# Value tiles copied out of PSUM by ScalarE, the x1 spread moved to ScalarE and its maxima to the next body

## What is computed

```python
x = x + tanh(g_xattn) * mha(layernorm(x), ctx, ctx, Wq, bq, Wk, bk, Wv, bv, Wo, bo)
x = x + tanh(g_ffn)   * ffn(layernorm(x), clip_x, clip_down, w_gate, w_up, w_down)

# mha: v = ctx @ Wv.T + bv;  o = softmax(q k / sqrt(32)) @ v;  result = o @ Wo.T + bo
# ffn: xq = fake_quant(x, clip_x)      scale = sigmoid(clip_x) * max|x| / 127 over the whole tensor
#      h  = fake_quant(silu(xq @ Wg.T) * (xq @ Wu.T), clip_down);  result = h @ Wd.T
```

## Time and profile before

| what | value |
|---|---|
| median of three runs | 1910.21 us (1909.71 to 1914.14) |
| the profiled execution | 1910.74 us, its span 1909.0 us |
| busy over the span | PE 88%, DVE 76%, ACT 45%, POOL 26% |
| granted TensorE clock, mean | 0.970 |
| chain that ended last | issue 38%, PE 31%, DVE 16%, POOL 8%, DMA 5%, ACT 2% |
| costliest lines of VectorE | L842 304.4 us (256), L834 224.6 us (128) |
| start, 14 steady bodies, body 15 and last body, weights, feed-forward | to 107; to 1211; to 1336; to 1383; to the end |

### The profile page before, as it was taken

How to read it: one execution, slowest core, us unless ns; L and a number is a source line. 1 busy time by engine, 2 the same in 40 slices (tenths; PEclk the granted TensorE clock), 3 DMA queues, 4 the chain that set the end, 5 groups by cost and what they waited for, 6 DMA issues and landing times.

```text
span 1909.0 us, 36308 instructions
## 1 busy us (share of the span) xinstructions
PE 1687.6 (88%) x12892; PEld 832.0 (44%) x12892; DVE 1441.6 (76%) x1917; ACT 866.3 (45%) x1036; POOL 497.3 (26%) x686
## 2 busy tenths in 40 slices
PE   3788999989999899998999989986599999989787
PEld 3354444544445444454444444433344444434333
DVE  6648788787786877868778687777877778878555
ACT  2243433434335343353443533414777777756242
POOL 6123323223232232322323223212000000006634
PEclk6999999999999999999999999999799999999899
DMA  5233332323323233233332332225235454115897
GB/s 187 67 109 92 88 105 73 110 87 88 109 81 101 87 86 112 84 94 105 84 100 85 91 107 61 78 56 199 94 121 210 165 203 150 45 45 213 337 419 296
DMA packets 132189, 239.73 MB, mean 126 GB/s; under 512 B 17456, under 2 KB 66608, under 8 KB 129584
## 3 DMA queue, kind: packets, MB, share of 16 engines
q1 hardware_dynamic: 132144, 239.14, 38.1%
HBM read 126.10 MB, written 62.39 MB: 99 GB/s over the span
## 4 chain that ended last, share of the span: by engine, by line
issue 38%; PE 31%; DVE 16%; POOL 8%; DMA 5%; ACT 2%; POOLq 0%; DVEq 0%; SPq 0%; ACTq 0%
PE bank L1244 11%; PE bank L1149 5%; PE bank L1151 5%; PE bank L1150 5%; PE spair L1226 4%; DMA x<-out_dram 4%; DVE mx L842 3%; POOL xl L485 3%; DVE rs L834 3%; POOL yh L559 3%; DVE xbuf L806 2%; DVE v L826 1%; ACT xh L580 1%; DVE ndev L866 1%; DVE parts L821 1%
## 5 line engine op out<-in xcount | busy, mean ns | idle before, releaser
L593 ACT ACTIVATE pr<-spair 128x1024 f32<-128x1024 f32 x256 | 259.2, 1020 | 142.1 <-PE spair L1226 142.1
L842 DVE TENSOR_REDUCE mx<-spair 128x4 f32<-128x1024 f32 x256 | 304.4, 1212 | 0.0
L834 DVE RECIPROCAL rs<-bank 128x256 f32<-128x256 f32 x128 | 224.6, 1755 | 56.5 <-PE bank L1244 56.1
L821 DVE SCALAR_TENSOR_TENSOR parts<-bank,bqk,parts 128x512 f16<-128x512 f32 x128 | 94.5, 747 | 132.5 <-ACT parts L586 132.5
L515 POOL TENSOR_TENSOR ol<-o,oh 128x256 f16<-128x256 f32 x128 | 86.5, 675 | 389.7 <-ACT oh L602 380.8
L586 ACT ACTIVATE parts<-bank,bqk 128x512 f16<-128x512 f32 x128 | 88.0, 687 | 219.9 <-PE bank L1151 219.9
L1355 PE MATMUL spair<-xqT,wgT 128*128 128x512 bf16 x704 | 181.9, 381 | 1.2 <-ACT xqT L703 1.2
L1355 PE MATMUL spair<-xqT,wuT 128*128 128x512 bf16 x704 | 181.7, 381 | 0.0
L1244 PE MATMUL bank<-pr,v 128*32 128x256 f32 x2048 | 138.1, 387 | 27.2 <-DVE o L836 27.2
L1226 PE MATMUL spair<-stacks 128*128 128x256 f16 x1024 | 152.5, 275 | 6.5 <-DMA stacks<-mT 6.2
L686 ACT ACTIVATE sil<-spair,gsc 128x512 f32<-128x512 f32 x176 | 118.2, 680 | 74.9 <-PE spair L1355 74.9
(11 more groups left out here) (172 smaller groups left out, 3408.8 us busy)
## 6 DMA issues: line engine op xcount, KB each, us to landing
stacks<-parts SPq DMA_DIRECT2D x768, 64.0 KB, 2.0
x<-out_dram SPq DMA_DIRECT2D x32, 1024.0 KB, 11.0
h_spill<-hb SPq DMA_DIRECT2D x10, 2816.0 KB, 9.2
hb<-h_spill SPq DMA_DIRECT2D x10, 2816.0 KB, 15.6
xbuf<-in_x_dram SPq DMA_DIRECT2D x16, 1024.0 KB, 5.3
cbuf<-in_ctx_dram SPq DMA_DIRECT2D x16, 1024.0 KB, 5.3
xres<-in_x_dram SPq DMA_DIRECT2D x16, 1024.0 KB, 5.2
out_dram<-xres SPq DMA_DIRECT2D x16, 1024.0 KB, 4.3
```

The lines of the kernel that those rows point to most:

```text
L593: act.activation(pr[:, u % 4, :, :, :].rearrange("p a b q -> p (a b q)"), spair[u % 2][:, :, :].rearrange("p a q -> p (a q)"), ACT.Exp, sc ...
L821: dve.scalar_tensor_tensor(out=parts[:, c, 2 * w + 1, :], in0=pj[g % 3][:, :], scalar=bqk[:, w, c:c + 1], in1=parts[:, c, 2 * w, :], op0=A ...
L834: dve.reciprocal(rs[:, g % 2, :], obank[:, S:2 * S]).then_inc(recip_done, 1)
L842: dve.tensor_reduce(mx[:, h:h + 2, b, :], spair[u % 2][:, :, :].rearrange("p a (q k) -> p a q k", q=KH), AX_X, ALU.max).then_inc(max_done, 1)
```

## The change

It has two halves. First, the bias of the value projection no longer goes into v. At the start of the kernel `value_bias` (VectorE, eight small instructions) spreads bv into a high and a low half, TensorE multiplies them by Wo (12 matmuls into `obank`), and `output_bias` adds the product to `tgbo`. `v_copy` becomes a scaled copy on ScalarE, behind the last `o_high` and ahead of ch. Second, x1's spread goes to ScalarE as `spread(before, g)`, one tile in each of the slots 0 to 3 of the next body, with the absolute value; its maxima go to VectorE as `x1_top`, one tile in each of the slots 1 to 4 of that body. `x1_spread` keeps shift and scale. GpSimd's bias additions to `xres` go from the head of its body to one ahead of each `o_low` of slots 4 to 7. The first body stands outside of the loop on ScalarE and VectorE, since it has no group before. The last group's spread stands behind the first two weight roundings on ScalarE, and the integer rounding of the second weight behind the maxima on VectorE. SP's program has the same rows but for the load of bv, now a column.

```diff
-            sp.dma_start(bvb[:, :], bv.partition_broadcast(P)).then_inc(bias_in, 16)
+            sp.dma_start(bqk[:, 2, :], bv.rearrange("(c p) -> p c", p=P), allow_slow_non_contiguous=True).then_inc(bias_in, 16)
...
             def body(j, nxt):
-                residual(j)
                 for g in range(NGR):
+                    if g >= NT:
+                        residual(j, g - NT)
                     o_low(j, g)
...
+            def v_copy(i, t):
+                wait(act, v_mm, i * NT + t + 1)
+                act.activation(v[:, t, :], pj[(2 + t) % 3][:, :], ACT.Copy, scale=1.0 / WS).then_inc(v_ready, 1)
+
+            def spread(j, t):
+
+                wait(act, x1_shift, 2 * j + 2)
+                wait(act, x1_max, j * NT)
+                at = bass.ds(j * NT + t, 1)
+                act.activation(ndev[:, t, :], xres[:, t, :], ACT.Abs, scale=rstd2[:, at], bias=shift2[:, at]).then_inc(x1_dev, 1)
...
                     if g > 0:
                         o_high(j, g - 1)
+                    if g < NT and before is not None:
+                        spread(before, g)
                 o_high(j, NGR - 2)
                 o_high(j, NGR - 1)
+                if i is not None:
+                    for t in range(NT):
+                        v_copy(i, t)
...
             weight_round(0)
             weight_round(1)
+            for t in range(NT):
+                spread(NG - 1, t)
             weight_copies(0)
...
-            def v_copy(i, t):
-                wait(dve, v_mm, i * NT + t + 1)
-                dve.scalar_tensor_tensor(out=v[:, t, :], in0=pj[(2 + t) % 3][:, :], scalar=1.0 / WS,
-                                         in1=bvb[:, :], op0=ALU.mult, op1=ALU.add).then_inc(v_ready, 1)
...
+            def value_bias():
+
+                for c in range(KC):
+                    dve.tensor_scalar(bvr[:, 0, c, :], ones32[:, :], bqk[:, 2, c:c + 1], None, ALU.mult).then_inc(bv_hi, 1)
+                for c in range(KC):
+                    wait(dve, bv_hi, c + 1)
+                    dve.scalar_tensor_tensor(out=bvr[:, 1, c, :], in0=ones32[:, :], scalar=bqk[:, 2, c:c + 1],
+                                             in1=bvr[:, 0, c, :], op0=ALU.mult, op1=ALU.subtract).then_inc(bv_lo, 1)
+
+            def output_bias():
+                wait(dve, bo_mm, 1)
+                dve.scalar_tensor_tensor(out=tgbo[:, :], in0=obank[:, :], scalar=small[:, TGX16:TGX16 + 1], in1=tgbo[:, :],
+                                         op0=ALU.mult, op1=ALU.add).then_inc(bo_ready, 1)
...
-                for t in range(NT):
-                    dve.tensor_scalar(ndev[:, t, :], xres[:, t, :], mv2[:, t, 0:1], r2[:, t:t + 1],
-                                      ALU.subtract, ALU.mult).then_inc(x1_dev, 1)
                 at = bass.ds(j * NT, NT)
...
-                wait(dve, x1_dev, j * NT + NT)
-                dve.tensor_reduce(amax2[:, at], ndev[:, :, :], AX_X, ALU.max,
-                                  apply_absolute_value=True).then_inc(x1_max, 1)
...
+            def x1_top(j, t):
+                wait(dve, x1_dev, j * NT + t + 1)
+                dve.tensor_reduce(amax2[:, bass.ds(j * NT + t, 1)], ndev[:, t, :], AX_X, ALU.max).then_inc(x1_max, 1)
...
+                    if 1 <= g <= NT and before is not None:
+                        x1_top(before, g - 1)
...
+            for t in range(NT):
+                x1_top(NG - 1, t)
+            dve.wait_ge(x1_max, NG * NT)
             dve.tensor_reduce(small[:, M1:M1 + 1], amax2[:, :], AX_X, ALU.max).then_inc(m1_part, 1)
+            weight_int(1)
...
+            pe.wait_ge(bv_lo, KC)
+            three(obank[:, :], [([bvr[:, s, k, :] for s in range(2)], [wT[3][:, k, s, :] for s in range(2)])
+                                for k in range(KC)]).then_inc(bo_mm, 1)
             turns(1, range(8), (v_ready, 2))
+            pe.wait_ge(bo_ready, 1)
             turn_max(0)
```

More of the change, by code:

```diff
@@ L71, in gated_block_kernel @@
         (GX, GF, CX, CD, TGX, TGX256, TGF, M1, M1A, SIGX, SIGD, SX, INVX, M2, M2A, SH, INVH,
-         CDN, EX, ED, EX1, ED1, S1, S2) = range(24)
+         CDN, EX, ED, EX1, ED1, S1, S2, TGX16) = range(25)
         p1 = ExitStack()
@@ L204, in gated_block_kernel @@
         x1_max = sem("x1_max")
+        x1_shift = sem("x1_shift")
+        bv_hi = sem("bv_hi")
+        bv_lo = sem("bv_lo")
+        bo_mm = sem("bo_mm")
+        bo_ready = sem("bo_ready")
         fw_in = [sem(f"fw_in{m}") for m in range(3)]
@@ L516, in o_low, with residual @@
                                    ALU.subtract).then_inc(o_lo, 1)
-            def residual(j):
+            def residual(j, t):
                 wait(pool, res_in, j * 16 + 16)
-                for t in range(NT):
-                    pool.tensor_tensor(xres[:, t, :], xres[:, t, :], tgbo[:, :], ALU.add).then_inc(res_bias, 1)
+                pool.tensor_tensor(xres[:, t, :], xres[:, t, :], tgbo[:, :], ALU.add).then_inc(res_bias, 1)
             def x1_rstds(j):
@@ L631, in _, with body @@
             turn_copies(1, range(TM | 1, 8, 2))
-            def body(i, j, nxt):
+            def body(i, j, before, nxt):
                 if i is not None:
@@ L655, in body @@
                     turn_copies(nxt, range(TM | 1, 8, 2))
[L657 to L660, removed]
+            body(1, 0, None, 2)
+            with act.Fori(2, NG - 1) as i:
+                body(i, i - 1, i - 2, i + 1)
+            body(NG - 1, NG - 2, NG - 3, None)
+            body(None, NG - 1, NG - 2, None)
             def weight_round(m):
@@ L757, in constants @@
                 dve.tensor_scalar(tgbo[:, :], tgbo[:, :], small[:, TGX:TGX + 1], None, ALU.mult).then_inc(const_done, 1)
[L758 removed]
+                dve.tensor_scalar(bqk[:, 0:2, :], bqk[:, 0:2, :], WS, None, ALU.mult).then_inc(const_done, 1)
+                dve.tensor_scalar(small[:, TGX16:TGX16 + 1], small[:, TGX:TGX + 1], 1.0 / WS, None, ALU.mult).then_inc(const_done, 1)
                 dve.wait_ge(sig_exp, 2)
@@ L909, in _, with body @@
             x_moments(1)
-            for t in range(NT):
-                v_copy(0, t)
-                if t < 2:
-                    key_max(0, 12 + 2 * t)
-                    key_max(0, 13 + 2 * t)
+            for u in range(12, 16):
+                key_max(0, u)
+            output_bias()
             x_prep_norm(1)
             prep_turns(1, 1)
-            def body(i, j, nxt):
+            def body(i, j, before, nxt):
                 if i is not None:
@@ L971, in body @@
                     weight_scale(2, 2 * IC + 1)
-                    weight_int(1)
                 x1_spread(j)
-            with dve.Fori(1, NG - 1) as i:
-                body(i, i - 1, i + 1)
-            body(NG - 1, NG - 2, None)
-            body(None, NG - 1, None)
-            dve.wait_ge(x1_max, NG)
+            body(1, 0, None, 2)
+            with dve.Fori(2, NG - 1) as i:
+                body(i, i - 1, i - 2, i + 1)
+            body(NG - 1, NG - 2, NG - 3, None)
+            body(None, NG - 1, NG - 2, None)
+            for t in range(NT):
+                x1_top(NG - 1, t)
+            dve.wait_ge(x1_max, NG * NT)
             dve.tensor_reduce(small[:, M1:M1 + 1], amax2[:, :], AX_X, ALU.max).then_inc(m1_part, 1)
+            weight_int(1)
             def down_copies():
```

20 lines of the change are left out of this document (10 added, 10 removed).

## The result

| | before | after |
|---|---|---|
| median of 12 runs | 1910.62 us (1908.62 to 1914.14) | 1915.43 us (1913.44 to 1918.07) |
| profiled execution, its span | 1910.74, 1909.0 | 1917.92, 1915.9 |
| granted TensorE clock, mean | 0.970 | 0.959 |
| VectorE, ScalarE busy over the span | 76%, 45% | 72%, 49% |

The ratio is 1.0025 [1.0017, 1.0033]: 4.8 us slower, where 1910.4 had been forecast in a range of 1902 to 1919. It lies within the 0.3% that was called no change, at its slow side; the interval leaves out 1, so the 4.8 us are real.

The account below looks back on a forecast made before the run. TensorE was taken to bound steady bodies only where no wait shows, with VectorE full in the tail. 19.0 + 4.2 + 2.05 - 25.1 = +0.2 us on 1910.74, median 0.5 below that: 1910.4 us, range 1902 to 1919.

Parts of the forecast that it names:

- Tail and head: Steady attention bodies: tail gains 1.25 us, head 0.51, over 14 bodies 24.6; with 0.5 in the last projecting body, 25.1.
- hand-over: Body's tail: time from a score pair's start to the next maximum's start, between 0.27 and 0.46 us, taken as 0.43.
- the body behind them: Last body with projections, after the 14 steady ones: loses its value tiles as well, gaining 0.5 us.
- The 0.90 for cl: Body's tail: a normalisation lengthened to 1.43 us across GpSimd's cl no longer meets it, gaining 0.90 us.
- Last body: Last attention body: gate weights leave 18.5 us later behind the residual load's wait for ScalarE's spreads, costing 19.0 us.
- The sum's small terms: Last body: two x1 maxima between later normalisations add 2 x 0.6 us; a wait in old order takes off 0.75.
- Start of the feed-forward part: ScalarE's last-group spreads delay the weight copies and third rounding, so VectorE's rounding of the third weight starts 4.2 us later.
- Start of the kernel: Before the second group's transposes: twelve bias matmuls and the bias addition delay VectorE's four normalisations, costing 2.05 us.
- Rival 1: Last body: TensorE at 1.2 GHz, fourth value product through output projection, adds about 2.5 and 5 us: 1918; chance 0.12.
- Rivals 2 to 5: Tail gain lost, 1928 (0.04); weights in time, 1891 to 1901 (0.07); hand-over 0.27, 1901 (0.09); middle slot/transfers, 1914 to 1919 (0.08).

Follow-up runs that it names:

- e7: Changed kernel, but in the 14 loop bodies ScalarE copies ch of the next group ahead of the four value tiles; 1928.51 us.
- e3: Changed kernel, but SP issues the gate and up weight loads ahead of the last residual's load; 1894.81 us.
- e10: Changed kernel with start ch ahead of value tiles, output bias behind layernorm tiles, weights ahead of last residual, last spread behind gate-weight copies; 1881.66 us.
- e8: Changed kernel, but on ScalarE the last group's spread stands behind the 11 gate-weight copies; 1909.78 us.
- e2: Changed kernel, but at the start ch is copied ahead of the value tiles and the output bias stands behind the four layernorm tiles; 1906.58 us.
- e11: Kernel before, with weight loads ahead of the last residual's load and GpSimd's bias additions each ahead of one of the last four low parts; 1912.12 us.
- e12: As e10, and SP waits until the last group's row of maxima has landed before issuing the gate weights; 1883.82 us.

## Why the prediction was right, and where it wasn't

It was right in total because two large terms were right and one small one was not. The small one took it near the edge: 0.3% is 5.7 us, and 4.8 were lost.

- **Tail and head, 25.1 forecast, 25.06 measured.** Body 77.05 forecast, 77.02 measured. The hand-over, for which no row stood, was taken as 0.43 and is 0.43: pair at 551.02, maximum at 551.45. The halves measured apart are 1.22 and 0.59 (1.25 and 0.51 forecast). That the sums agree to 0.04 is in part luck: the 14 bodies gave 1.80 each instead of 1.76, 25.2 in all, and the body behind them, which was to give 0.5, lost 0.2. The first value product after it took 1.83 us instead of 1.30. (Between the reciprocals at which I cut, the first body gave 2.90 and the fifteenth lost 1.25; 1.1 of each is where the cut stands, as a body's first reciprocal came late behind the four spreads in the kernel before, except in body 1.) The 0.90 for cl is the best supported: e7 puts it back and pays 1.03.
- **Last body, 19.0 forecast, 18.8 measured.** e3 takes 17.2 of it away with nothing but a place in SP's queue, and e10, whose last value product ran at full clock (e3's took 1.94 us), all 18.8. So the stall is the whole cost. The sum's small terms, 1.2 for x1's maxima less 0.75, don't show: e10 has the maxima too. VectorE's 17.74 us for the weights and the 0.29 and 0.64 for slow value products make 18.7 of the 18.8. The large term was right, that the total fits to 0.2 is in part luck.
- **Start of the feed-forward part, 4.2 forecast, 4.6 measured.** e8 gives back 4.7, so it was the order on ScalarE. TensorE's slow output projection delayed x1's second tile by 1.25 us, which wasn't in the term. From there to the rounding of the third weight it is 4.1 us longer than before (the forecast's 4.2), and from that to `csb` 0.8 shorter (1371.25 to 1382.34, before 1365.20 to 1377.05), which wasn't in it either.
- **Start of the kernel, 2.05 forecast, 5.1 measured to the first transposes, 7.5 to the first reciprocal in the profiled execution.** This is the mis-sized term. I followed VectorE's delay and took the rest of the chain as it was. But the value tiles moved to ScalarE ahead of ch there too. I had used just this in the loop, where it takes cl off the layernorm tiles; at the start it puts cl on them. The Trainium skill, SBUF — State Buffer, Who interferes with whom, calls the port pair that VectorE and GpSimd share an exclusive lock. The trace agrees: the tile that met cl ended 0.28 or 0.29 us behind it in four places (the start, e2's start, e7's loop, and the earlier trace rows). The same rule that I had applied to the loop I didn't apply at the start.
- **Rival 1, the clock in the last body, 1918.** Its condition didn't come: the product at 1315.48 and the last one ran in 1.07 us. Part of its price did. The value products at 1309.42 and 1321.16 ran slow, mostly but not wholly covered by VectorE, which waited 0.29 and 0.64 us for them (0.75 in the kernel before, for its one); the output projection lost 1.25 us of the 5 priced.
- Rivals 2 to 5 fell: cl and xl had 1.9 us of slack, the weights were not in time, the hand-over was 0.43, and the bodies had no unexplained part over 0.03 us.

The forecast was 0.2 us slower than the kernel before, and 4.8 were measured. Of the 4.6 between, 3.0 is the collision and 0.4 the feed-forward start; the last body gives 0.2 back. The rest, 1.4, is below the scatter of the clock at the start, which some executions with this start show (62.67, 62.32) and others don't (60.36, 60.27). That it is this scatter is not shown, since each kernel has one profiled execution.

## What to carry to other kernels

An instruction that goes to another engine pushes everything behind it there; follow that in every copy of the code, in the prologue and the last pass as well as in the loop, since the same shift can part two instructions in the one and join them in the other. In a one-way queue of DMA issues look at what stands behind each wait: one load whose release came 18 us later cost three quarters of what the bodies had gained, and one exchanged line gave it back. Before exchanging, look at who waits for the load that is now last, since the same exchange cost 11 us in the kernel where its reader stood at the head of GpSimd's body, 8.7 of them for that reason.

## What the runs showed of the hardware that I had not expected

- Kernels with one and the same program up to a place can differ there by 2.4 us from one execution to another. After 5 to 12 us without work TensorE got 2.4 GHz back during transposes alone in all 14 profiles (0.63 to 0.39 us for four). In 4 of them the granted clock fell to 0.50 again around a wait of 2.27 us, and twelve matmuls took 4.4 us instead of 2.75.
- A 16 KB transfer took 1.0 us longer to land for two loads of 2.8 MB issued right behind it (5.2 against 4.2), and a 1 MB load took 18.1 us behind them (e11) instead of 5.6 (before).
- The first value product of the last body, which comes soon after TensorE's wait for the row of maxima, took 1.20, 1.30, 1.83, 1.86 or 1.94 us (e10, before, after, e12, e11) after waits of 7.24, 6.19, 6.20, 6.21 and 7.16 us: the length of the wait alone doesn't tell which.
- GpSimd's cl held up only VectorE's layernorm tile. In the kernel before, the maxima at 552.02 and 553.76 and the value tile at 553.16 ran while cl did (551.81 to 556.03) and took their usual 1.22, 1.21 and 0.68 us.
